# Two parts of a chunked attention kernel in other shapes: the gate's first product as 256-column matmuls, the state in 64x64 blocks

## The reference, cut to what matters

```python
q, k, v = x @ Wq, x @ Wk, x @ Wv        # 16 heads of 32
q, k = rotate(silu(q)), rotate(silu(k))
def step(S, qkv):                       # chunks of 128 rows, S is 32x32 per head
    scores = einsum('bthd,bshd->bhts', qi, ki) * D[None]
    o_intra = einsum('bhts,bshd->bthd', scores, vi)
    o_inter = einsum('bthd,bhde->bthe', qi * decay_q, S)
    S_new = lam_C * S + einsum('bshd,bshe->bhde', ki * decay_k, vi)
gate = x @ Wg1 @ Wg2                    # Wg1 is 512x32, Wg2 is 32x512
o = group_rmsnorm(o * sigmoid(gate)) * weight
x = x + o @ Wo
```

## Time and profile before

| | |
|---|---|
| three runs | 1288.71, 1288.82, 1288.97 us (median 1288.82) |
| profiled execution, its own time | 1288.75 us |
| its span | 1286.7 us |
| PE busy in the span | 1270.3 us (99%) |
| DVE, ACT, POOL busy | 917.0 us (71%), 475.2 us (37%), 435.2 us (34%) |
| TensorE clock granted | 1.0 of full in the whole span |

### The profile page before, as it was taken

The page is one execution under the profiler, slowest core; times in us unless marked ns, Lnnn a source line. Parts: engine busy times, 40 slices in busy tenths (PEclk is TensorE's granted clock), DMA queues, the critical chain, the costliest instruction groups (busy, mean ns, idle before and its releaser), DMA issues.

```text
span 1286.7 us, 20699 instructions
## 1 busy us (share of the span) xinstructions
PE 1270.3 (99%) x7376; PEld 1043.5 (81%) x7376; DVE 917.0 (71%) x1594; ACT 475.2 (37%) x799; POOL 435.2 (34%) x360
## 2 busy tenths in 40 slices
PE   9999999998999999999999999999999999999998
PEld 6888888887788888888888888888888888888887
DVE  7878788788867667676767676767767666767665
ACT  5433434434433333333333433333333333333421
POOL 2434455564442322223132324133232324232400
PEclk9999999999999999999999999999999999999999
DMA  9000000000001000010000000001001000000003
GB/s 326 12 2 1 19 17 2 2 1 2 25 25 33 17 33 27 22 33 28 29 24 24 24 24 24 33 16 33 24 24 33 24 33 24 24 24 24 24 13 119
DMA packets 21778, 40.23 MB, mean 31 GB/s; under 512 B 2660, under 2 KB 2916, under 8 KB 21604
## 3 DMA queue, kind: packets, MB, share of 16 engines
q1 hardware_dynamic: 21060, 39.47, 9.4%
q10 hardware_dynamic: 672, 0.13, 0.1%
HBM read 35.40 MB, written 4.19 MB: 31 GB/s over the span
## 4 chain that ended last, share of the span: by engine, by line
PE 93%; DVE 2%; POOL 1%; ACT 1%; issue 1%; POOLq 0%; DVEq 0%; ACTq 0%
PE bank L1351 16%; PE bank L1354 15%; PE bank L1353 15%; PE bank L1197 13%; PE bank L1199 13%; PE bank L1198 13%; PE bank L1211 2%; PE bank L1291 1%; PE bank L1310 1%; PE bank L1300 1%; PE bank L1343 1%; PE bank L1331 1%; PE bank L1258 0%; ACT xg L394 0%; PE bank L1257 0%
## 5 line engine op out<-in xcount | busy, mean ns | idle before, releaser
L883 DVE TENSOR_TENSOR acc<-acc,bank 128x512 f32<-128x512 f32 x248 | 169.3, 683 | 129.4 <-PE bank L1199 129.3
L1197 PE MATMUL bank<-wdh,hh 128*128 128x512 f32 x512 | 199.3, 389 | 0.0
L1199 PE MATMUL bank<-wdh,hl 128*128 128x512 f32 x512 | 199.2, 389 | 0.0
L1198 PE MATMUL bank<-wdl,hh 128*128 128x512 f32 x512 | 199.2, 389 | 0.0
L1351 PE MATMUL bank<-xoh,wgh 128*128 128x512 f32 x448 | 175.9, 393 | 0.6 <-DVE cxa L891 0.6
L1351 PE MATMUL bank<-xoh,wuh 128*128 128x512 f32 x448 | 175.1, 391 | 0.7 <-ACT cxa L482 0.7
L1354 PE MATMUL bank<-xoh,wgl 128*128 128x512 f32 x448 | 174.5, 390 | 0.0
L1354 PE MATMUL bank<-xoh,wul 128*128 128x512 f32 x448 | 174.3, 389 | 0.0
L1353 PE MATMUL bank<-xol,wuh 128*128 128x512 f32 x448 | 174.3, 389 | 0.0
L1353 PE MATMUL bank<-xol,wgh 128*128 128x512 f32 x448 | 174.3, 389 | 0.0
L899 DVE TENSOR_TENSOR hl<-hx,hh 128x512 fp32r<-128x512 f32 x128 | 113.5, 887 | 51.4 <-ACT hh L489 51.0
(11 more groups left out here) (163 smaller groups left out, 2285.7 us busy)
## 6 DMA issues: line engine op xcount, KB each, us to landing
stg<-packed_dram SPq DMA_DIRECT2D x48, 256.0 KB, 2.5
stg<-scales_dram SPq DMA_DIRECT2D x48, 256.0 KB
out_dram<-acc SPq DMA_DIRECT2D x16, 256.0 KB, 2.0
acc<-x_dram SPq DMA_DIRECT2D x3, 1024.0 KB, 15.0
w_in<-wq_dram SPq DMA_DIRECT2D x2, 512.0 KB, 5.2
w_in<-wk_dram SPq DMA_DIRECT2D x2, 512.0 KB, 6.9
w_in<-wv_dram SPq DMA_DIRECT2D x2, 512.0 KB, 8.6
w_in<-wo_dram SPq DMA_DIRECT2D x2, 512.0 KB, 11.2
```

The costliest lines, as they stand in the source:

```text
L883: V.tensor_tensor(row, row, BY[j % 2][:], ALU.add).then_inc(y_add, 1)
L1197: pe.matmul(dst, w_h, x_h, start=start, stop=False)
L1198: pe.matmul(dst, w_h, x_l, start=False, stop=False)
L1199: return pe.matmul(dst, w_l, x_h, start=False, stop=stop)
```

## The change

`gate1` multiplies with high and low x in one go: both lie in one tensor (`xt`, and `ot` for tile 1), so that a matmul moves 256 columns (128 of high, 128 of low x) and there are 4 of them instead of 8. The two sums come out beside each other and have to be added: ACT copies the first to `gs` (`gate_copy`), DVE adds the second (`sum_gate`), and `gate_low` on both engines then works from `gs`. PE's scores wait for `gate_sum`.

The state is kept in blocks of two heads: 64x64, with zeros outside the two 32x32 diagonal blocks. `inter` and `kv_product` issue 8 matmuls each. `state` has two instructions in place of one, each of 256 columns, which multiply the product by a 0/1 column (`halfT`); `scaled` works on 256 columns instead of 128. One more table is loaded.

```diff
@@ buffers
-            st = sb("st", [P, KT, HD], F32, att)
+            st = sb("st", [P, KT, 2 * HD], F32, att)
...
+            xth, xtl = xt[:, 0, :, :], xt[:, 1, :, :]
+            oth, otl = ot[:, 0, :, :], ot[:, 1, :, :]
@@ sync
             sp.dma_start(lamT[:], lam_c).then_inc(s_tab, 16)
+            sp.dma_start(halfT[:], half).then_inc(s_tab, 16)
             sp.dma_start(maskT[:], mask.rearrange("p r g t -> p r (g t)")).then_inc(s_tab, 16)
@@ scalar
             def gate_low(t):
+                act.wait_ge(gate_sum, t + 1)
+                act.wait_ge(gate_ps, t)
+                A(g4h[96:128, :], gs[96:128, 1, :], ACT.Copy)
+                A(g4[0:96, :], gs[0:96, 1, :], ACT.Copy).then_inc(g_hi, 1)
+
+            def gate_copy(t):
+
                 act.wait_ge(g1_ps, t + 1)
-                act.wait_ge(gate_ps, t)
-                A(g4h[96:128, :], BS[3][96:128, 0:P], ACT.Copy)
-                A(g4[0:96, :], BS[3][0:96, 0:P], ACT.Copy).then_inc(g_hi, 1)
+                act.wait_ge(gate_sum, t)
+                A(gs[:, 0, :], BS[3][:, 0:P], ACT.Copy).then_inc(g1_sb, 1)
...
                 silu_qk(t + 1)
-                gate_low(t + 1)
+                gate_copy(t + 1)
                 if at_start(b, c):
                     xt_hi_(2)
+                gate_low(t + 1)
                 v_copy(t + 1, (c + 1) % 2)
@@ vector
+            def sum_gate(t):
+
+                dve.wait_ge(g1_sb, t + 1)
+                dve.wait_ge(g_hi, t)
+                V.tensor_tensor(gs[:, 1, :], gs[:, 0, :], BS[3][:, P:2 * P], ALU.add
+                                ).then_inc(gate_sum, 1)
...
-                if c:
-                    V.tensor_tensor(st[:], st[:], kv, ALU.add).then_inc(st_done, 1)
-                else:
-                    V.tensor_copy(st[:], kv).then_inc(st_done, 1)
+                for v in range(2):
+                    cols = slice(HD * v, HD * v + HD)
+                    kv = src[:, 0:KT * 2 * HD].rearrange("p (g d) -> p g d", g=KT)[:, :, cols]
+                    if c:
+                        ins = V.scalar_tensor_tensor(out=st[:, :, cols], in0=kv,
+                                                     scalar=halfT[:, v:v + 1], in1=st[:, :, cols],
+                                                     op0=ALU.mult, op1=ALU.add)
+                    else:
+                        ins = V.tensor_scalar(st[:, :, cols], kv, halfT[:, v:v + 1], None, ALU.mult)
+                ins.then_inc(st_done, 1)
...
                 decayed_q(t)
-                gate_low(t + 1)
+                sum_gate(t + 1)
                 if at_start(b, c):
                     xt_lo_(2)
+                gate_low(t + 1)
                 rope_of(b, c, t + 1, (c + 1) % CHUNKS)
@@ tensor, gate1
-                    pe.matmul(BS[3][:, 0:P], g1, xh[:, k, :], start=(k == 0), stop=False)
-                    ins = pe.matmul(BS[3][:, 0:P], g1, xl[:, k, :], start=False,
-                                    stop=(k == KT - 1))
+                    ins = pe.matmul(BS[3][:, 0:2 * P].rearrange("p (a t) -> p a t", a=2),
+                                    g1s[:, k, :, :].rearrange("p r d -> p (r d)"), x[:, :, k, :],
+                                    start=(k == 0), stop=(k == KT - 1))
@@ tensor, inter
-                    for r in range(QB):
-                        rows = slice(HD * r, HD * r + HD)
+                    for v in range(2):
+                        rows = slice(2 * HD * v, 2 * HD * v + 2 * HD)
@@ tensor, kv_product
-                    for r in range(QB):
-                        head = slice(HD * (QB * g + r), HD * (QB * g + r) + HD)
-                        ins = pe.matmul(dst[HD * r:HD * r + HD, HD * g:HD * g + HD], kd[:, head],
-                                        vs[:, c % 2, head], start=True, stop=True)
+                    for v in range(2):
+                        w = 2 * HD
+                        heads = slice(w * (2 * g + v), w * (2 * g + v) + w)
+                        ins = pe.matmul(dst[w * v:w * v + w, w * g:w * g + w], kd[:, heads],
+                                        vs[:, c % 2, heads], start=True, stop=True)
@@ tensor, tile
-                pe.wait_ge(g_lo, t + 2)
+                pe.wait_ge(gate_sum, t + 2)
```

More of the change, by code:

```diff
@@ L74, in shape_constants @@
     decay_k = np.exp(lam[None, :] * (P - 1.0 - i[:, None])).astype(f)
+    half = np.repeat(np.tile(np.eye(2, dtype=f), (2, 1)), HD, axis=0)
     lam_c = np.repeat(np.exp(lam * P).reshape(KT, QB).T, HD, axis=0).astype(f)
@@ L77, in shape_constants @@
     return {"rot": c(rot), "mask": c(mask), "decay_q": c(decay_q), "decay_k": c(decay_k),
-            "lam_c": c(lam_c), "ident": np.eye(P, dtype=f)}
+            "lam_c": c(lam_c), "half": c(half), "ident": np.eye(P, dtype=f)}
 def build(nc, x, wq, wk, wv, wo, wg1, wg2, norm_w, packed, scales,
-          rot, mask, decay_q, decay_k, lam_c, ident, out):
+          rot, mask, decay_q, decay_k, lam_c, half, ident, out):
     ctx = ExitStack()
@@ L119, in build @@
             xn = sb("xn", [P, 512], F32, att)
-            xth = sb("xth", [P, KT, P], F32R, att)
+            gs = sb("gs", [P, 4, P], F32, att)
             sq = sb("sq", [P, 512], F32, att)
-            oth = sb("oth", [P, KT, P], F32R, att)
+            kd = sb("kd", [P, 512], F32, att)
             wo_h = sb("wo_h", [P, KT, 512], F32R, att)
@@ L212, in build @@
         qk_ps, g1_ps, v_ps, gate_ps = sem("qk_ps"), sem("g1_ps"), sem("v_ps"), sem("gate_ps")
+        g1_sb, gate_sum = sem("g1_sb"), sem("gate_sum")
         g_hi, g_lo = sem("g_hi"), sem("g_lo")
@@ L355, in xt_hi_ @@
                 if t == 1:
-                    A(oth[:], BO[:].rearrange("p (k t) -> p k t", k=KT), ACT.Copy
+                    A(oth, BO[:].rearrange("p (k t) -> p k t", k=KT), ACT.Copy
                       ).then_inc(xt_hi, 1)
@@ L360, in xt_hi_ @@
                     act.wait_ge(v_ps, 1)
-                    A(xth[:], BO[:].rearrange("p (k t) -> p k t", k=KT), ACT.Copy
+                    A(xth, BO[:].rearrange("p (k t) -> p k t", k=KT), ACT.Copy
                       ).then_inc(xt_hi, 1)
@@ L364, in xt_hi_ @@
                 act.wait_ge(v_ps, t)
-                A(xth[:], BV[:].rearrange("p (k t) -> p k t", k=KT), ACT.Copy).then_inc(xt_hi, 1)
+                A(xth, BV[:].rearrange("p (k t) -> p k t", k=KT), ACT.Copy).then_inc(xt_hi, 1)
             def gate_low(t):
+                act.wait_ge(gate_sum, t + 1)
[3 more added lines that the diff above has]
+            def gate_copy(t):
                 act.wait_ge(g1_ps, t + 1)
-                act.wait_ge(gate_ps, t)
-                A(g4h[96:128, :], BS[3][96:128, 0:P], ACT.Copy)
-                A(g4[0:96, :], BS[3][0:96, 0:P], ACT.Copy).then_inc(g_hi, 1)
+                act.wait_ge(gate_sum, t)
+                A(gs[:, 0, :], BS[3][:, 0:P], ACT.Copy).then_inc(g1_sb, 1)
             def silu_qk(t):
@@ L403, in ot_hi_ @@
                 act.wait_ge(wo_ps, t)
-                A(oth[:], BO[:].rearrange("p (k t) -> p k t", k=KT), ACT.Copy).then_inc(ot_hi, 1)
+                A(oth, BO[:].rearrange("p (k t) -> p k t", k=KT), ACT.Copy).then_inc(ot_hi, 1)
             def wide_hi(k, n, dst, piece):
@@ L429, in _ @@
             silu_qk(0)
+            gate_copy(0)
             xt_hi_(1)
@@ L500, in passage @@
                 silu_qk(t)
+                gate_copy(t)
                 gate_low(t)
@@ L672, in xt_lo_ @@
                 if t == 1:
[L673 to L674 removed]
+                    V.tensor_tensor(otl, BO[:].rearrange("p (k t) -> p k t", k=KT),
+                                    oth.bitcast(F32), ALU.subtract).then_inc(xt_lo, 1)
                     return
                 if t == 2:
[L677 to L678 removed]
+                    V.tensor_tensor(xtl, BO[:].rearrange("p (k t) -> p k t", k=KT),
+                                    xth.bitcast(F32), ALU.subtract).then_inc(xt_lo, 1)
                     return
[L680 to L681 removed]
+                V.tensor_tensor(xtl, BV[:].rearrange("p (k t) -> p k t", k=KT),
+                                xth.bitcast(F32), ALU.subtract).then_inc(xt_lo, 1)
+            def sum_gate(t):
[3 more added lines that the diff above has]
+                                ).then_inc(gate_sum, 1)
             def gate_low(t):
                 dve.wait_ge(g_hi, t + 1)
[L685 removed]
+                V.tensor_tensor(g4[96:128, :], gs[96:128, 1, :], g4h[96:128, :].bitcast(F32),
                                 ALU.subtract).then_inc(g_lo, 1)
@@ L709, in ot_lo_ @@
                 dve.wait_ge(ot_hi, t + 1)
-                V.tensor_tensor(otl[:], BO[:].rearrange("p (k t) -> p k t", k=KT),
-                                oth[:].bitcast(F32), ALU.subtract).then_inc(ot_lo, 1)
+                V.tensor_tensor(otl, BO[:].rearrange("p (k t) -> p k t", k=KT),
+                                oth.bitcast(F32), ALU.subtract).then_inc(ot_lo, 1)
             def add_x1(t):
@@ L787, in _ @@
             dve.wait_ge(s_rot, 16)
+            sum_gate(0)
             rope_of(None, 0, 0, 0)
```

(16 more changed lines are left out.)

9 lines of the change are left out of this document (4 added, 5 removed).

## The result

The changed kernel takes 1291.65 us (median of 20 runs, 1290.81 to 1293.15), beside 1288.97 us for the kernel before in 20 runs on the same chips. The ratio is 1.0019, 95% interval [1.0012, 1.0025]: slower by 0.1 to 0.3%. The profiled execution took 1290.81 us, with a span of 1289.0, 2.3 more than before.

A forecast was written before the change was run, and what follows sets the result against it. The prediction took PE, 93% of the chain, to bound the kernel. Its terms, -4.73 + 0.80 + 0.20 + 0.10 = -3.6 us, on a profiled 1288.75 with the median 0.07 above, gave 1285.2 us; range 1281.5 to 1290.0.

The forecast's parts named there:

- who can use the saving: Gate product's 0.43 us saving reaches PE in eleven tiles, 4.73 us gained; rotation 0.61 later, 0.21 idle left before `ot_lo_`.
- gate1: Gate's first product on PE: four 256-column matmuls at 0.12 us, the piece costing 0.71 us, a saving of 0.43.
- Wide moves cost double: Rival, chance 0.05: 256-column matmuls in the gate's first product take 0.22 us, no gain, about +1.1 us, 1289.9.
- Tiles 1, 8 and 10: Tiles where DVE comes last: sum 0.89 us later; gain 0.17, loss 0.86, loss 0.11 respectively, together a loss of 0.80.
- the signs: Expected in the new profile, among others: PE's wait before tile 8's output product near 1.5 us.
- The start and the passage: Gate products of tiles 0 and 15: savings end in PE's waits for POOL's rotation (start) and DVE (passage).
- inter: State product `inter` on PE: 16 records, half the instructions on half the strips, 1.01 us as before, no change.
- both rivals on it: `inter` cheap, 0.5 us saved each time, 1280 us, chance 0.10; `inter` dear, 1.0 more each time, 1298 us, chance 0.13.
- kv_product: PE's kv product: grows at most 0.2 to 0.3 us, covered by the ACT wait except in tile 0; charged 0.2.
- State: DVE's two state instructions, 256 columns, about 0.41 us each, ending 277.55; 0.1 us charged for tile 13 and passage together.
- The table: Extra DMA on SP's queue before the mask: 0.7 us taken, within 1.5 us of cover, so no cost.
- The longer route eats the gain: Rival, chance 0.17: gate's copy, sum and hand-overs take 0.9 to 1.1 us instead of 0.61; 1286.5 to 1289.

The follow-up runs named there:

- the shifted kernel: Kernel before with three small throwaway DVE operations ahead of `gate_low`, delaying the rotation; 1291.43 us, ratio 1.0016.
- the gate reordered: Changed kernel with the state edits undone, DVE doing the rotation right behind the sum and `gate_low` after the masks (at the start, rotation before sum); 1290.30 us.
- state alone: Kernel before plus only the state edits (`st`, `state`, `scaled`, `inter`, `kv_product`) and the table; 1290.10 us, ratio 1.0007.
- the gate alone: Changed kernel with state edits and table undone, only the gate's first product new; 1294.24 us, ratio 1.0037. In pairs: the same undoing plus that pair's moves.
- POOL after norm: Changed kernel, DVE's order moved, second weights' low part earlier, POOL's half-rotation waiting for the previous tile's norm; 1284.43 us without state edits, 1285.15 with.
- DVE reordered: Changed kernel, rotation right behind the sum, `gate_low` after the masks, at the start rotation before sum; 1292.18 us with state edits, 1290.30 without.
- three moves: Changed kernel, DVE's order moved, POOL's half-rotation (tiles 2 to 14) after DVE's, second weights' low part earlier; 1284.82 us without state edits, 1285.89 with.
- POOL after DVE: Changed kernel, POOL's half of the rotation in tiles 2 to 15 waiting for DVE's half; 1291.77 us, ratio 1.0018.

## Why the prediction was wrong

**The step that failed** is in "who can use the saving": "Idle before `ot_lo_` is 1.25 us there: 1.25 - 0.61 - 0.43 = 0.21 stays". The delay was right: the rotation starts 156.51 - 153.67 = 2.84 us after gate1 instead of 155.23 - 153.00 = 2.23, so 0.61 later. What was wrong is that its 1.52 us went into the sum as a fixed duration. It was in part a wait already: alone it takes 1.22. With the durations of before, the sum should have read: asked at 155.23 + 0.61 = 155.84, POOL's second instruction begun at 155.67 and 1.31 long, ending at 156.98, and 1.08 more is 158.06, for 156.75 before. That is 1.31 later, not 0.61, and 1.25 - 1.31 - 0.43 = -0.49: the whole gain of 0.43 is eaten. Measured: -0.02 to -0.09 in nine of the eleven tiles. Tile 0, which has no output product, kept its 0.43, and tile 5, the eleventh, lost 0.28, since there it was the gate's low part that was held (1.24 for 0.29). Together the eleven gained 0.74 us for a forecast of 4.73: that is 4.0 of the 5.9 us between the forecast's sum (-3.6) and what the traces show at tile 15 (+2.26).

The row that should have raised the question stood in the trace of before: POOL's second instruction at 2.27 beside its first at 1.31, and the rotation at 1.52 in some tiles, 1.27 or 1.82 in others.

The Trainium skill has the rule, and I hadn't used it. "SBUF — State Buffer", section "Who interferes with whom", says that a DVE instruction with two SBUF inputs contends with a GpSimd instruction that reads SBUF, that the ports they share are an exclusive lock, and that issue order decides who blocks. The traces agree: in tile 7 the rotation takes the rest of POOL's present instruction and 1.08 us (1.52 before, 2.19 after, 2.13 in the shifted kernel, 2.06 with the gate reordered), and so do all 128 rotations that were held. By the same rule the new `gate_low` was a risk, as it now reads both operands from SBUF (`gs`, `g4h`), where before one came from PSUM: 0.29 when free, 0.34 in most tiles, where POOL's first instruction ends 0.2 us after it asks, but 1.37, 1.06, 1.24, 1.07 and 1.07 in tiles 0, 1, 5, 10 and 14, where before it was 0.30. The sum, with one operand in PSUM, was never held: 0.27 to 0.29, in tile 7 too, where all of it lies inside POOL's first instruction.

**gate1**: 0.70 for a forecast of 0.71. Right. "Wide moves cost double" was wrong.

**Tiles 1, 8 and 10**: forecast +0.80 together, measured 0.45 + 0.66 + 0.65 = 1.76. Tile 8 lost 0.66 of the 0.86 forecast, by the route predicted. PE's wait there is 1.02; the 1.5 written among the signs doesn't follow from the prediction's own terms (0.22 + 0.86 = 1.08). Tiles 1 and 10 lost to the held `gate_low`, 0.77 each beyond its free length.

**The start and the passage** were wrong. I let the saving end in waits there at no cost. At the start the sum stands ahead of the rotation, so POOL's instruction gets the first turn: the rotation takes 2.04 (1.23 before), and the low part of the second weights, which now meets POOL's sum, 1.59 (0.68 before). PE waits 0.66 and 0.61 where it waited 0.66 in all; the first transposes come 0.64 later. In the passage the norm of tile 13 is late (a step ahead of it is held, 0.76 for 0.21) and PE, which arrives earlier, waits 1.12 instead of 0.47.

**inter**: 1.02 for 1.01 in 16 records. Right, and both rivals on it wrong. Its price of 126 ns for one record alone was read too high, without effect on the result: record by record, a group of four (now of two) starts together, and the next group 0.109 us later; the rest of the 1.01 is the longer step of about 0.2 from the last group to intra's first.

**kv_product**: right. It is longer and later after intra, the time until ACT's copy is ready covers it, and in tile 0 it costs 0.18 (state alone) for a forecast of 0.20.

**State**: I gave its two instructions 256 columns each. They have 128 each, 0.59 us for the pair, as in tile 13, after:

```profile
278.20 0.59 DVE L847 SCALAR_TENSOR_TENSOR st<-bank,halfT,st 128x128 f32<-128x128 f32 x2
278.97 0.69 DVE L720 TENSOR_REDUCE ms<-sq 128x16 f32<-128x512 f32 x1 [0.18 <-ACT sq L410]
```

They cost nothing there. (By the prediction's own 0.41 each they would have ended at 277.61, not 277.55.) But the state's part as a whole was priced too low. Between the gate alone and both (POOL after norm) tile 15 starts 0.95 us later, from tiles 10 and 14 (0.42 and 0.43), against a forecast of 0.30 for all of the state. In the other pairs it is 1.03 (state alone against before), 1.07 (DVE reordered) and 0.56 (three moves); only between the gate alone and the full change is it 1.82 the other way, since there the held newton step and norm of tile 1 don't occur. The ratios of the last pair (0.9962 and 0.9961) can't tell a difference. What in the state's part costs this wasn't tried.

**The table**: no wait came of it, as forecast.

**The rivals.** "The longer route eats the gain" had the result in ordinary tiles and the place, but its mechanism (slow copies and hand-overs) was wrong: those took the 0.61 forecast. It ended at 1289 since it too left out the start, the passage and the held `gate_low`. The slower side, a dear inter, was the wrong mechanism. What was missing was a rival in which an instruction's duration depends on when it asks.

## What to carry to other kernels

A duration from a trace is not always the work of the instruction. Before a DVE instruction with two SBUF inputs is moved, look at what POOL does at its old and its new time, and compute its end from the end of POOL's instruction; where durations of one form differ (1.22, 1.52, 1.27), it has been waiting. When PE or ACT gets faster, POOL's instructions that they release move too and may fall on something small and critical, like a newton step. It can be cheaper to hold POOL back by one semaphore than to let it start early, and an instruction that waits for another engine should not stand ahead of one whose turn must be had early.

## What was not expected of the hardware

An operation of 16 columns is held as long as one of 1024: 1.20 us for 0.17, twice in a row, as POOL's second instruction begins before DVE's next asks. An instruction that POOL's half of the rotation holds ends its free length less 0.14 us after POOL's: the rotation 1.08 (1.22 free), the norm 0.55 (0.69), the gate's low part 0.15 (0.29), a newton step 0.03 (0.17). It isn't only tensor with tensor: a dequantisation step with one tensor and constants (TENSOR_SCALAR of 512 int32) took 2.22 us beside POOL's weight parts in the kernel with POOL after DVE, and the next one of the kind, after POOL, 0.41; the kernel before has one of 2.22, too, at 200.40. One wait can prevent others: with POOL held back for the norm, DVE's tiles 1, 8 and 10 shortened by 2.0, 2.0 and 2.2 us against the reordered kernel.

A matmul that moves 256 columns of fp32r costs 0.12 us here, and one that moves 128 costs 0.11. Sixteen records on two 64x64 tiles take as long (1.02 us) as 32 on four 32x32 tiles (1.01): in both shapes eight groups follow each other, 0.109 us apart.
